# DRAM arrays in 2 KB pieces, one forward-transform pass for both images, and another order of units in a Fourier-operator kernel

## What is computed

```python
h = einsum('bhwi,ic->bhwc', x, fc0_w) + fc0_b          # 3 -> 64 channels
for l in range(4):
    xf = rfft2(h)                                       # keep 32 x 16 modes
    top = einsum('bixy,ioxy->boxy', xf[:, :, :16, :16], w1[l])
    bot = einsum('bixy,ioxy->boxy', xf[:, :, -16:, :16], w2[l])
    sc = irfft2(of)                                     # of: top and bot, zeros elsewhere
    y = sc + einsum('bihw,oi->bohw', h, pw_w[l]) + pw_b[l]
    h = gelu(batch_norm(y) * gamma[l] + beta[l])        # mean, variance over b, h, w
out = gelu(h @ fc1_w + fc1_b) @ fc2_w + fc2_b
```

## Time and profile before

| | us |
|---|---|
| median of 3 runs | 4752.23 (4751.26 to 4759.73) |
| the profiled execution | 4746.3 |
| its span | 4744.5 |
| fusion of layer 0 / 1 / 2 | 287 to 1180 / 1366 to 2225 / 2410 to 3250 |
| mixing of layer 0 / 1 / 2 / 3 | 112 to 287 / 1180 to 1366 / 2225 to 2410 / 3250 to 3430 |
| last fusion with fc1, fc2 / token blocks | 3430 to 4072 / 4072 to 4744 |

### The profile page before, as it was taken

How to read it: one execution, slowest core, us unless ns; L and a number is a source line. 1 busy time by engine, 2 the same in 40 slices (tenths; PEclk the granted TensorE clock), 3 DMA queues, 4 the chain that set the end, 5 groups by cost and what they waited for, 6 DMA issues and landing times. The chain is left out here.

```text
span 4744.5 us, 143699 instructions
## 1 busy us (share of the span) xinstructions
PE 3513.1 (74%) x65092; PEld 2052.3 (43%) x65092; DVE 2431.2 (51%) x2474; ACT 2252.6 (47%) x2644; POOL 173.3 (4%) x249
## 2 busy tenths in 40 slices
PE   6768878886756777775757777775599999468877
PEld 4634444443633444443634444444444444353432
DVE  4644444443555666654656666664533333364556
ACT  3634444453644545444635555454466666222322
POOL 2022000000000000000000000000000101100000
PEclk8879988898878888888878889888799999669778
DMA  8756454546767667666767677768734332003043
GB/s 301 278 140 172 126 129 112 130 108 215 268 181 212 194 205 217 201 199 224 248 197 216 196 212 221 206 187 286 263 133 158 139 145 89 11 1 64 10 86 68
DMA packets 162317, 800.22 MB, mean 169 GB/s; under 512 B 26889, under 2 KB 33361, under 8 KB 111854
## 3 DMA queue, kind: packets, MB, share of 16 engines
q1 hardware_dynamic: 150876, 776.16, 54.2%
q0 software_dynamic: 7936, 13.65, 0.9%
q10 hardware_dynamic: 2898, 1.17, 0.1%
HBM read 448.68 MB, written 342.23 MB: 167 GB/s over the span
## 5 line engine op out<-in xcount | busy, mean ns | idle before, releaser
L822 PE MATMUL bank<-fb,arena 64*64 64x128 f32 x16384 | 699.0, 310 | 342.7 <-issue 236.1
L822 PEld LDWEIGHTS bank<-fb,arena 64*64 64x64 f32 x16384 | 613.2, 199 | 640.0 <-issue 584.3
L1034 ACT ACTIVATE arena<-bank 128x1024 f32<-128x1024 f32 x384 | 393.0, 1023 | 888.9 <-PE bank L954 546.3
L839 DVE TENSOR_TENSOR arena<-bank,arena 128x1024 f32<-128x1024 f32 x384 | 466.2, 1214 | 523.8 <-PE bank L822 523.2
L1079 DVE STREAM_TRANSPOSE arena<-arena 128x1024 f32<-128x1024 f32 x384 | 470.3, 1225 | 210.4 <-ACT arena L1024 203.3
L954 PE MATMUL bank<-arena,wst 64*64 64x512 f32 x3072 | 471.8, 672 | 36.3 <-issue 27.2
L831 DVE STREAM_TRANSPOSE arena<-bank 128x1024 f32<-128x1024 f32 x256 | 317.2, 1239 | 271.3 <-PE bank L812 271.3
L970 PE MATMUL bank<-arena,fwq 32*32 32x256 f32 x12288 | 329.6, 403 | 145.7 <-issue 141.4
L1027 ACT ACTIVATE arena<-arena,shift,scale 128x1024 f32<-128x1024 f32 x256 | 316.3, 1235 | 240.5 <-DVE arena L839 240.5
L1086 DVE STREAM_TRANSPOSE arena<-bank 128x1024 f32<-128x1024 f32 x192 | 237.6, 1237 | 375.5 <-PE bank L970 375.5
L1041 ACT ACTIVATE arena<-arena 128x1024 f32<-128x1024 f32 x384 | 402.4, 1048 | 0.7
(11 more groups left out here) (238 smaller groups left out, 3740.3 us busy)
## 6 DMA issues: line engine op xcount, KB each, us to landing
y_dram<-arena SPq DMA_DIRECT2D x192, 1024.0 KB, 11.1
arena<-y_dram SPq DMA_DIRECT2D x96, 2048.0 KB
arena<-spec_in SPq DMA_DIRECT2D x32, 2048.0 KB, 8.8
spec_out<-arena SPq DMA_DIRECT2D x128, 512.0 KB, 8.2
arena<-in_w_modes SPq DMA_DIRECT2D x28, 2048.0 KB, 14.0
arena<-spec_out SPq DMA_DIRECT2D x112, 512.0 KB, 15.1
spec_in<-arena SPq DMA_DIRECT2D x24, 2048.0 KB, 8.6
spec_in<-arena SPq DMA_DIRECT2D x4, 4096.0 KB, 13.7
```

Source lines behind the costliest of these rows:

```text
L822: mm = pe.matmul(hpx(bank[2 * s + i][CHAN[v], :])[:, :, j * S:(j + 1) * S], a2[p % 2][CHAN[i], :, v, 4 * T + j], hpx(fb2[CHAN[i], :]), sta ...
L839: dve.tensor_tensor(chunk(p, T), slot(s), chunk(p, T), ALU.add).then_inc(y_added, 1)
L1034: act.activation(chunk(p, T), slot(NEXT_SLOT[T]), ACT.Copy).then_inc(evicted, 1)
```

## The change

Three things change at once.

1. **Layout in DRAM.** `spec_in` and `spec_out` get the group of images ahead of the partition, `y_dram`, `w_even` and `w_modes` are cut into blocks of `BK` = 512 numbers with the partition inside: one contiguous run is 2 KB for one partition. The loads and stores name the same data and the same on-chip tiles; their pieces are now 2 KB throughout. The store of a plane is four DMAs of 64 partitions and 512 KB, where it was two of 1 MB. The first stage stores its spectra in eight DMAs instead of four.
2. **Forward transforms.** `w_dft(p)` does both images with 32 matmuls of 512 columns, using all of banks 4 to 7, so that nothing waits between the images; `w_turn` reads columns i * 256 onwards. `h_dft` uses 32 x 64 tiles: 32 matmuls of 256 columns with both halves of a table in one. Its result lies in another order of partitions, and `store_spectra` puts it right with four DMAs of 32 partitions instead of one of 128.
3. **Order.** TensorE, ScalarE and VectorE take their units in another order, y quarter 2 moves to slot 0 (`Y_SLOT`), and the waits that guard the slots are rewritten for it.

The core of the diff:

```diff
+    out["w_modes"] = np.ascontiguousarray(out["w_modes"].reshape(L, NCH, P, MC * C // BK, BK).transpose(0, 1, 3, 2, 4))
...
-        spec_in = nc.dram_tensor("spec_in", [NCH, P, NG, MC * GI], F32, kind="Internal").ap()
-        spec_out = nc.dram_tensor("spec_out", [NCH, P, NG, 2, GI * C // 2], F32, kind="Internal").ap()
-        y_dram = nc.dram_tensor("y_dram", [NP, P, PX], F32, kind="Internal").ap()
-        w_even = nc.dram_tensor("w_even", [L, P, K1 * C], F32, kind="Internal").ap()
+        spec_in = nc.dram_tensor("spec_in", [NCH, NG, P, MC * GI], F32, kind="Internal").ap()
+        spec_out = nc.dram_tensor("spec_out", [NCH, NG, P, GI * C], F32, kind="Internal").ap()
+        y_dram = nc.dram_tensor("y_dram", [NP, PX // BK, P, BK], F32, kind="Internal").ap()
+        w_even = nc.dram_tensor("w_even", [L, K1 * C // BK, P, BK], F32, kind="Internal").ap()
...
         def load_weights(sp, l, c):
-            sp.dma_start(w_sb[c % 3], d["w_modes"][l, c]).then_inc(w_loaded[c % 3], 16)
+            sp.dma_start(by_block(w_sb[c % 3]), d["w_modes"][l, c].rearrange("t p x -> p t x")).then_inc(w_loaded[c % 3], 16)
...
         def load_pair(sp, l, p):
-            sp.dma_start(pb[p % NS], y_dram[p].rearrange("p (i x) -> p i x", i=2)).then_inc(p_loaded[p % NS], 16)
+            sp.dma_start(pb[p % NS].rearrange("p i (t x) -> p (i t) x", x=BK), y_dram[p].rearrange("t p x -> p t x")).then_inc(p_loaded[p % NS], 16)
...
-        Y_SLOT = (0, 1, 1, 0)
+        Y_SLOT = (0, 1, 0, 0)
...
                 for i in range(2):
-                    sp.dma_start(y_dram[p].rearrange("(v c) (i x) -> i c v x", v=2, i=2)[i], pb[p % NS][CHAN[i]]).then_inc(p_stored[p % NS], 16)
+                    for v in range(2):
+                        sp.dma_start(y_dram[p, 4 * i:4 * i + 4, CHAN[v]].rearrange("t c x -> c t x"),
+                                     pb[p % NS][CHAN[i], v].rearrange("c (t x) -> c t x", x=BK)).then_inc(p_stored[p % NS], 16)
...
-                sp.dma_start(spec_in[:, :, g].rearrange("h p x -> p h x"), xs.rearrange("p h m k b -> p h (m k b)")).then_inc(spec_stored, 16)
+                for v in range(2):
+                    for ro in range(2):
+                        to, at_ = ro * C + v * HB, v * C + ro * HB
+                        sp.dma_start(spec_in[:, g, to:to + HB].rearrange("h p x -> p h x"),
+                                     xs[at_:at_ + HB].rearrange("p h m k b -> p h (m k b)")).then_inc(spec_stored, 16)
...
                 if T == 2:
-                    if p > 0:
-                        pe.wait_ge(evicted, n * 4)
+                    if p < NP - 1:
+                        pe.wait_ge(rows_turned, n * 2 + 3)
...
-                if T < 2:
+                if T == 0:
+                    pe.wait_ge(drained, n * 4 + 3)
+                if T == 1:
                     if p < NP - 1:
-                        pe.wait_ge(rows_turned, n * 2 + 3 + T)
+                        pe.wait_ge(rows_turned, n * 2 + 4)
...
-                            mm = pe.matmul(bank[4 + g][QUAD[c], 0:256], fwq[QUAD[g], s * 32:(s + 1) * 32],
-                                           hT[p % 2][QUAD[g], i, :, s, c * CQ:(c + 1) * CQ],
+                            mm = pe.matmul(bank[4 + g][QUAD[c], :], fwq[QUAD[g], s * 32:(s + 1) * 32],
+                                           hT[p % 2][QUAD[g], :, :, s, c * CQ:(c + 1) * CQ].rearrange("p i h c -> p (i h) c"),
                                            start=(s == 0), stop=(s == 1), tile_position=(32 * g, 32 * c))
...
-                    for j in range(4):
-                        ro, v = j // 2, j % 2
-                        col = (k * 2 + ro) * K1
+                    for v in range(2):
                         for c in range(4):
-                            mm = pe.matmul(bank[4 + c][QUAD[j], 256:512], ghq[QUAD[c], col:col + K1],
+                            mm = pe.matmul(bank[4 + c][CHAN[v], 256:512], ghq[QUAD[c], k * 2 * K1:(k + 1) * 2 * K1],
                                            t1[p % 2][QUAD[c], hh * 2 + v, :, :, ri * M2:(ri + 1) * M2],
-                                           start=(k == 0), stop=(k == 3), tile_position=(32 * c, 32 * j))
+                                           start=(k == 0), stop=(k == 3), tile_position=(32 * c, C * v))
```

More of the change, by code:

```diff
@@ L1061, in scalar_fuse @@
                     gelu(n, 2)
-                    evict(n, 0)
                 if before:
@@ L1107, in vector_fuse @@
                     add(n, 1)
+                if after:
+                    turn_rows(dve, l, n + 1, 0, ROWS_SLOT[0])
+                if now:
                     px_turn(n, 0)
```

108 lines of the change are left out of this document (54 added, 54 removed).

## The result

The changed kernel takes 4379.9 us (median of four, 4370.6 to 4389.8) against 4751.7 for the kernel before, timed beside it: a ratio of 0.922, 95% interval 0.919 to 0.925. The profiled execution has a span of 4374.7 us, 369.8 less than before. The forecast was 4330 us, 422 less; its range, and the range of its own case, hold the measured time. Its sum was nearly right, its terms less so, and the experiments are about that.

What follows compares the result with a forecast made beforehand. TensorE's waits for late code were taken to bound the fusions. Layers 1 and 2 -307 us, layer 0 -106, mixings -32, starts +12, last spectra +11 sum to -422: about 4330 us as a median, range 4140 to 4620.

Steps and rivals of the forecast that it cites:

- its own case: The forecast's likeliest outcome, held at 54%: about 4330 us, range 4220 to 4440, with steady passes of 19.5 to 22.5 us.
- What bounds the kernel: In the fusions TensorE waits for late instruction code: 163 us of stops in layer 1, plus an echo through a lower clock.
- Matmuls: Forward transforms in the fusions: w_dft saves 1.0 us, h_dft 0.7, less 0.2 for wider weights; 1.5 us a pass.
- Code: Steady passes: 2.6 code packets for 3.7, each costing 0.8 us of stop for 1.4; saves 2.1 us, plus 1.0 of echo.
- Order: The new order of TensorE's units against their waits: some 0.3 us gained and as much lost, 0 within 1 a pass.
- Transfers: DMA time of a steady pass by counted rates: 16.9 us before, 18.4 after.
- the floor of 19 us: Steady passes can't go under 19 us of DMA time; with 19.3 us of other work beside it, 21.0 was taken.
- the slower case: 2 KB pieces stored from 64 partitions may pay per piece, making passes DMA-bound: about 5000 us at 100 GB/s; 5%.
- Mixing: Four mixings: smaller pieces take 8 of L605's 20.6 us of stops off each, -32 us in all (0 to -60).
- Boundaries: Starts of mixings and fusions 1.5 us longer, eight times, +12; last group's spectra 9.2 for 5.5 us, three times, +11.
- The signs in the profile: Expected: 2048 records per transform a stage, near 420 packets, 21 us passes, 70 us issue waits, DMA share 0.9, clock above 0.9.
- The first rival: Code waits are not shortened, since bytes queued ahead and not their pieces delay a fetch: 4545 us; 23%.

Runs made afterwards that it cites:

- old_order: The new layout and new transforms with the old order of units, the one w_dft where its first half stood; 4429 us, 0.933 of the kernel before.
- no_layout: The changed kernel with the layout hunks taken back; 4430 us, 0.933 of the kernel before.
- planes_only: The changed kernel with row spectra issued a pass earlier and the old layout for weights, even planes and both spectra; 4235 us, 0.891 of the kernel before.

## Why the forecast came out, point by point

**What bounds the kernel** was right: the time was in TensorE's waits for code in the fusions and their echo in the clock, and taking blocks and DMA time away shortened them in every run.

**Matmuls, 1.5 us a pass: right in sum.** In an undisturbed pass of the changed kernel the w_dft holds TensorE for 2.28 us (1579.45 to 1581.73; forecast 1.8, before 2.9) and the h_dft for 1.91 (1397.08 to 1398.99; forecast 2.0, before 2.7): together 1.4 saved, the h_dft a little more than forecast and the w_dft 0.6 for 1.0. The units and those behind them, whose starts end the count:

```profile
1397.08 1.98 PE L999 MATMUL bank<-arena,ghq 32*64 32x256 f32 x64
...
1398.99 1.09 PE L973 MATMUL bank<-arena,wst 64*64 64x512 f32 x8
```
```profile
1579.45 2.35 PE L986 MATMUL bank<-arena,fwq 32*32 32x512 f32 x64
1581.73 1.95 PE L973 MATMUL bank<-arena,wst 64*64 64x512 f32 x16
```

The shortest steady passes are 16.7 to 17.4 us against a forecast of 16.2.

**Code, 0.8 us a packet: the number of packets right (425, forecast near 420), the price near, the reason not.** The changed kernel shows 0.7, and 1.0 with the rows in time. But the forecast gave the whole fall to the smaller pieces, and the layout alone brought 1.2 for 1.5; the rest came with the new transforms, which need fewer packets in a pass (old_order 0.7). Its 1.4 for today was the three largest rows only, where all of them give 1.5. The bounds, 0 and 1.4, held; the middle was a guess without a row behind it. Nor did the forecast have a wait for VectorE among the stops: in the new order y0 waits 0.5 us a pass for the fourth add.

**Order, 0 within 1 us a pass: this step failed.** In layer 0 it is worth some 95 us against the old order with w_dft in one place and some 60 against w_dft in the other: 2 to 3 us a pass. In the steady layers it is worth 20 to 23 us once the rows are in time. I compared the units one by one (which wait of each is nearer) and not the chain next1, eviction, next2, eviction, gelu, y0, which closes once a pass; where its stops lie together they also cost clock. That is the most of why layer 0 gained 186 us and not 106.

**Transfers: the floor of 19 us was right in kind, what it did was missed.** The y store from 64 partitions in 2 KB pieces runs as fast as the forecast took it:

```profile
1320.00:1324.00 4.00, 3.15 (x74) 2.33 (x78) 2.79 (x3) 3.61 (x6) 0.00 (x0) 1.00 0.94 225
```

so the mechanism of the slower case is absent. Two limits so close add to each other, I wrote, and took 1.7 us a pass for it without a place. The place is the last quarter of the row spectra, seven times a steady stage at 11.5 us, 80 / 32 = 2.5 us a pass. The forecast listed what else is issued on the SP queue but did not ask how long a transfer lies behind a pair's store and load, nor that the new order asks for the first rows sooner. Where this wait is gone, a pass takes 20.0 us, less than the 21.0 forecast.

**Mixing, -32 us: wrong.** The largest issue row of the mixing of layer 1 is 16.3 us in five stops, for 20.6 in ten, but the mixings as a whole became 10 us longer, and with the old layout (no_layout) they were 712 us. The pieces of weights and spectra shorten no wait that mattered there. Nor do they alone make the mixings longer: planes_only has the old pieces for both and still 733. What does is open.

**Boundaries.** The last group's spectra were taken at 3.7 us more each. After layer 0 the time from their issue to the first load of the mixing is 18.3 us; before it was 7.3. The SP queue before, then after:

```profile
1144.67 1.24 SPq L853 DMA_DIRECT2D y_dram<-arena  x2
1160.73 0.38 SPq L868 DMA_DIRECT2D spec_in<-arena  x1
1168.02 1.28 SPq L519 DMA_DIRECT2D arena<-spec_in  x3
```

```profile
970.52 7.23 SPq L860 DMA_DIRECT2D y_dram<-arena  x4
980.48 7.27 SPq L879 DMA_DIRECT2D spec_in<-arena  x4
998.76 5.46 SPq L524 DMA_DIRECT2D arena<-spec_in  x3
```

The last y store is issued 10 us ahead of them and takes 9.2 us by the earlier trace rows; before, 16 us lay between. After layers 1 and 2 the time is 15.2 and 17.0 us, for 10.3 and 7.4 before. After layer 1 the store was issued 15.4 us ahead, so a store in front of the spectra is at most a part of it. No run tried this by itself, and the cause is open.

**The signs in the profile.** As said: 2048 records of each transform in a stage (6144 in three), near 420 packets, 72 us of waits on issue for 70, passes of 21.6 us for 21. Not as said: a DMA share of 0.79 for 0.9, a clock of 0.88 for above 0.9, and the stores of the spectra, which landed after 7.2 us in layer 1 (median of the smaller DMAs) and not later than the 8.6 of before. The first two were the sign that something other than code and bytes made TensorE wait. The first rival (stops unchanged per packet, 4545 us) is wrong in price and time: a packet costs 0.7 to 1.0 us, not 1.4.

The sum was right because two errors stood against each other, and that was luck: layer 0 gave 80 us more, most of it through the order, and steady layers, mixings, ends and the stages outside gave some 130 less (34 + 47 + 36 + 11 + 4). The late rows are the largest cause of that: with them in time the steady fusions take 50 and 56 us less.

## What to carry to other kernels

When an order of units is changed, follow the chain of waits that closes once a pass, and look for two stops that come close together: here they cost their length and the clock after it. When a kernel gets faster, ask of every transfer that is issued just in time how many bytes are queued ahead of it, and issue it a pass sooner if its buffer is free; here one moved line gave another 118 us. Ahead of reshaping a DMA, look at the outer dimension of both its sides, and try the shape in a kernel of its own.

## What the hardware showed that was not expected

- With the rows in time a packet of code costs 0.4 us of stop with the DMA engines half busy (share 0.54), 0.7 at 0.80 and a full-rate store, and 1.0 at 0.85. With the same bytes queued, the shorter time of the DMA engines alone took a quarter of it away.
- In layer 0 of the changed kernel a stop of 2.35 us in every pass goes with a granted clock of 0.96; with another of 1.27 us, 1.1 us ahead of it, in the old order, the stage is granted 0.92, and in the pass shown the matmuls that follow run at half speed.
- "Issue" in these rows is not always code: stops of one and the same length (0.54, 1.26 or 2.37 us) that come once a pass and end 0.10 us after an instruction of VectorE or ScalarE are waits for that engine.
- DMAs with a destination of 2 x 64 x 512 kept to 2 of the 16 DMA engines: 52 GB/s, and a kernel 1.64 times as long as the same one with four stores from 64 partitions (6866 against 4190 us).
